# Row maxima of an attention score, taken from two PSUM banks by one VectorE instruction instead of two

## The reference

```
q = _lin(xn, Wq, bq).reshape(b, n, H, HD) / np.sqrt(HD)
k = _lin(xn, Wk, bk).reshape(b, n, H, HD)
score = jax.nn.softmax(jnp.einsum('bihd,bjhd->bhij', q, k), axis=-1)
v = _lin(xn, Wv, bv).reshape(b, n, R, HD)
out = jnp.einsum('bhij,bjrd->bihrd', score, v)
qv = _lin(xn, Wqv, bqv).reshape(b, n, H, 1, QK) / np.sqrt(QK)
comp = softmax(concatenate([qv, out], axis=-1) @ Ws.T + bs, axis=3)
out = (comp * out).sum(axis=3).reshape(b, n, DIM)
```

## Time and profile before

| what | value |
|---|---|
| median of 3 runs | 1427.76 us (1419.58 to 1430.48) |
| the profiled execution | 1429.73 us, span in the trace 1428.0 us |
| TensorE matmul | busy 1368.9 us (96%), 6333 instructions |
| VectorE | busy 1026.9 us (72%), 2050 instructions |
| GpSimd | busy 841.1 us (59%), 433 instructions |
| ScalarE | busy 756.1 us (53%), 1463 instructions |
| DMA | 48.35 MB, mean 34 GB/s |

### The profile page before, as it was taken

One profiled execution on the slowest core, in us unless ns is written; L12 is line 12 of the kernel. 1 busy time (PEld: TensorE's weight loads), 2 busy tenths in 40 slices (PEclk: granted clock), 3 DMA queues, 4 the chain that ended last, 5 costly groups with the idle time before them and its releaser, 6 DMA issues. The chain is left out here.

```text
span 1428.0 us, 23930 instructions
## 1 busy us (share of the span) xinstructions
PE 1368.9 (96%) x6333; PEld 436.7 (31%) x6333; DVE 1026.9 (72%) x2050; ACT 756.1 (53%) x1463; POOL 841.1 (59%) x433
## 2 busy tenths in 40 slices
PE   4699999999999999999999999999999999997898
PEld 3123222222222222222222222222222222223675
DVE  5745677877778686878777777768686868677852
ACT  4045555565555555555556555555555555563443
POOL 4235767576666766666757576665656565664321
PEclk9569999999999999999999999999999999999999
DMA  5200101010101001010101010100000000000000
GB/s 129 91 17 31 34 28 42 31 42 31 42 22 36 31 31 42 31 42 19 39 31 42 31 42 31 32 29 32 31 32 31 31 31 31 17 1 1 15 17 28
DMA packets 41937, 48.35 MB, mean 34 GB/s; under 512 B 4608, under 2 KB 23520, under 8 KB 41904
## 3 DMA queue, kind: packets, MB, share of 16 engines
q1 hardware_dynamic: 40770, 47.04, 10.0%
q0 software_dynamic: 352, 0.58, 0.3%
q10 hardware_dynamic: 782, 0.33, 0.1%
HBM read 22.51 MB, written 8.39 MB: 22 GB/s over the span
## 5 line engine op out<-in xcount | busy, mean ns | idle before, releaser
L1194 DVE TENSOR_REDUCE rowmax<-row_bank 128x1 f32<-128x512 f32 x1024 | 666.5, 684 | 319.9 <-PE row_bank L964 314.2
L1294 POOL TENSOR_TENSOR pair<-prob 128x1024 f32<-128x1024 f32 x256 | 603.8, 2359 | 452.0 <-ACT prob L1141 452.0
L1141 ACT ACTIVATE prob<-col_bank 128x512 f32<-128x512 f32 x1024 | 555.2, 594 | 463.9 <-PE col_bank L981 463.5
L989 PE MATMUL out_bank<-prob,v_op 128*64 128x512 f32 x2048 | 558.6, 624 | 0.0
L964 PE MATMUL row_bank<-k_op,q_op 72*128 72x512 bf16 x1024 | 323.6, 390 | 20.7 <-DMA v_op<-v_all 12.1
L981 PE MATMUL col_bank<-q_op,k_op 74*128 74x512 bf16 x1024 | 313.4, 387 | 0.1
L981 PEld LDWEIGHTS col_bank<-q_op,k_op 74*128 74x128 bf16 x1024 | 68.8, 98 | 332.2 <-ACT prob L1141 227.9
L989 PEld LDWEIGHTS out_bank<-prob,v_op 128*64 128x64 f32 x2048 | 101.9, 135 | 213.8 <-issue 200.5
L964 PEld LDWEIGHTS row_bank<-k_op,q_op 72*128 72x128 bf16 x1024 | 101.0, 99 | 167.6 <-DVE rowmax L1194 42.6
L999 PE MATMUL den_bank<-pair,onehot 128*32 128x512 f32 x1024 | 137.3, 608 | 0.0
L393 POOL TENSOR_TENSOR product<-mix_in,rows 128x2048 f32<-128x2048 f32 x16 | 72.5, 4529 | 2.1 <-POOLq L876 2.1
(11 more groups left out here) (183 smaller groups left out, 823.2 us busy)
## 6 DMA issues: line engine op xcount, KB each, us to landing
v_op<-v_all SPq DMA_DIRECT2D x64, 256.0 KB
k_op<-k_parts SPq DMA_DIRECT2D x64, 144.0 KB
q_op<-q_parts SPq DMA_DIRECT2D x192, 48.0 KB
q_parts<-along_parts SPq DMA_DIRECT2D x11, 192.0 KB, 2.2
k_parts<-along_parts SPq DMA_DIRECT2D x33, 64.0 KB, 2.1
out<-y_out SPq DMA_DIRECT2D x8, 256.0 KB, 2.3
q_op<-max_rows SPq DMA_DIRECT2D x64, 4.0 KB
q_parts<-first_parts SPq DMA_DIRECT2D x5, 192.0 KB, 2.1
```

What stands on the lines that cost most here:

```text
L989: last = nc.tensor.matmul(out_bank[slot % 2][ih * VW:(ih + 1) * VW, :], v_op[slot][:, t, :], halves(prob[:, t, :])[:, :, ih, :], start=(t ...
L1141: nc.scalar.activation(prob[:, t, h * HALF:(h + 1) * HALF], col_bank[h][:, :], ACT.Exp).then_inc(exp_done, 1)
L1194: nc.vector.tensor_reduce(rowmax[:, parity, t, h:h + 1], row_bank[h][:, :], AX.X, ALU.max).then_inc(max_done, 1)
L1294: pool.tensor_tensor(pair[:, k, :], prob[:, 2 * k, :], prob[:, 2 * k + 1, :], ALU.add).then_inc(pair_done, 1)
```

## The change

Both row banks become one PSUM tensor `row_banks` of 1024 columns (two banks), and `row_bank[0]` and `row_bank[1]` are its halves, so the matmuls write where they did. One `tensor_reduce` reads all 1024 columns and writes one maximum per query; it waits for both halves of the tile. `max_done` counts once per tile. TensorE waits once per tile, before the first half, that the reduction of tile t - 1 is done. `rowmax` loses its last dimension, so the reduction that negates the maxima reads 8 elements instead of 16. The steps of `split_max` come after the reduction: two of them after that of t = 0, one after that of t = 1.

```
-        rowmax = sb("rowmax", [P, 2, TB, 2])
+        rowmax = sb("rowmax", [P, 2, TB])
...
-        row_bank = [pb(f"row_bank{n}", [P, HALF]) for n in range(2)]
+        row_banks = pb("row_banks", [P, SEQ])
+        row_bank = [row_banks[:, n * HALF:(n + 1) * HALF] for n in range(2)]
...
             def row_scores(v, slot, t, known_free):
                 for h in range(2):
-                    if not known_free:
-                        pe.wait_ge(max_done, 2 * TB * v + 2 * t + h - 1)
+                    if not known_free and h == 0:
+                        pe.wait_ge(max_done, TB * v + t)
...
                         if last and (s, t) == (2, 0):
-                            pe.wait_ge(max_done, 2 * TB * U)
+                            pe.wait_ge(max_done, TB * U)
...
-            def row_max(v, parity, t, h):
-                dve.wait_ge(row_scored, 2 * TB * v + 2 * t + h + 1)
-                nc.vector.tensor_reduce(rowmax[:, parity, t, h:h + 1], row_bank[h][:, :], AX.X,
+            def row_max(v, parity, t):
+                dve.wait_ge(row_scored, 2 * TB * v + 2 * t + 2)
+                nc.vector.tensor_reduce(rowmax[:, parity, t:t + 1], row_banks[:, :], AX.X,
                                         ALU.max).then_inc(max_done, 1)
...
-                    dve.wait_ge(max_done, 2 * TB * w + 2 * TB)
-                    nc.vector.tensor_reduce(negmax[:, :], rowmax[:, parity, :, :], AX.X, ALU.max,
+                    dve.wait_ge(max_done, TB * w + TB)
+                    nc.vector.tensor_reduce(negmax[:, :], rowmax[:, parity, :].unsqueeze(2), AX.X, ALU.max,
                                             negate=True).then_inc(negmax_ready, 1)
...
-                        for h in range(2):
-                            if ahead:
-                                row_max(u + 2, s % 2, t, h)
-                            if 2 * t + h < 3 and not (last and s == SLOTS - 1):
-                                split_max(u + 1, (s + 1) % 2, 2 * t + h)
+                        if ahead:
+                            row_max(u + 2, s % 2, t)
+                        if not (last and s == SLOTS - 1):
+                            for step in {0: (0, 1), 1: (2,)}.get(t, ()):
+                                split_max(u + 1, (s + 1) % 2, step)
...
-                    for h in range(2):
-                        row_max(v, v, t, h)
+                    row_max(v, v, t)
```

## The result

The changed kernel takes 1473.59 us (median of 4 runs, 1469.45 to 1478.99), the kernel before beside it 1426.69; the ratio is 1.0337, with a 95% interval of 1.0284 to 1.039. The forecast was 1450 with a range of 1436 to 1466: right in sign, but the change cost 46.9 us where 22 were forecast. The profiled execution of the kernel after took 1478.99 us, with a span of 1477.2 against 1428.0.

The account below looks back on a forecast made before the run. It took TensorE to set the pace, VectorE counting only where TensorE waits for a bank. 8.4 us in the loop plus 13.6 ahead of group 0, 22.0, on 1429.73 gave 1451.7, taken as a median of 1450; range 1436 to 1466.

Parts of the forecast that it names:

- What bounds the kernel, and the margin of a plain tile: In the loop TensorE sets the pace; plain row pairs stay 1.98 us apart, the reduction fitting with 0.08 to spare.
- The merged reduction: One VectorE reduction of 1024 PSUM columns takes 1.21 us, as in SBUF, against 1.37 for two apart.
- Rival 3: Reading across two banks costs 1.37 us like two instructions, so every plain tile stalls 0.08: 1480 us, chance 0.10.
- The 82 us of VectorE's busy time: Over 512 merged reductions VectorE loses 82 us of busy time, 1.37 to 1.21 each, none on the path.
- Ahead of group 0: In the 16 tiles before group 0, matmuls and reduction form a chain, 2.34 us per tile against 1.42: 13.6 us more.
- The long steps: Around query part and weights TensorE's stalls grow 0.3 us each, 0.6 in each of 14 groups: 8.4 us.
- the 28 priced places: The query part and the weights in each of 14 groups, where TensorE stalls net 0.3 us longer.
- The two priced stalls of s = 2: Stalls at query part and weights: 0.6 and 0.61 us in along groups, against 0.32 each today; net 0.3 each.
- The clock: In group 0 the rise to 1.00 comes at the same work, first `denominators`, 13.6 us later, costing nothing further.
- Rival 2: The clock rises as soon as group 0 makes TensorE dense, 14.2 us less: 1436 us, chance 0.10.
- Rivals 4 and 5: 4: VectorE's saving reaches TensorE, 1414 us, chance 0.04. 5: the instruction is split again when built, chance 0.02.

Follow-up runs that it names:

- b1_sub_late: The kernel before, two reductions and two banks, with the subtraction of `split_max` behind the second row maximum of tile 1: 1445.71 us, ratio 1.015.
- a1_sub_ahead: The kernel after, with the subtraction of `split_max` ahead of the row maximum of tile 1 instead of behind it: 1447.19 us, ratio 1.0158.
- a5_all: The kernel after with early subtraction and the old start, plus query part, shift and weights ahead of their tiles' row maxima: 1537.28 us, ratio 1.0772.
- a6_sub_first: a5_all with the subtraction of `split_max` put ahead of the query part in tile 1: 1427.48 us, ratio 0.9993 to the kernel before.

## Why the prediction was wrong

- **What bounds the kernel, and the margin of a plain tile**: right. The loop grows by what TensorE's row pairs come late behind the held subtraction (0.74 us in the tile above), and plain row pairs in the kernel after stand 1.98 apart.
- **The merged reduction**, 1.21 us: right, 1.22. Rival 3, two banks as dear as two instructions, is out. The 82 us of VectorE's busy time that it was to save were too many, though: the two reductions of a pair overlap (1.29 us together, not 1.37), and the page's busy time goes from 666.5 to 625.2, 41 us.
- **Ahead of group 0**, 13.6 us: right, 13.9; undone by itself it came back.
- **The long steps**, 8.4 us: here it failed, in one sentence, "with the steps of `split_max` most are shorter" than the margin of 0.9. The subtraction was entered at 0.07 us, its price in its old place, though the change moves it from between two reductions to behind the merged one. In its new place it runs beside GpSimd's addition and lasts 1.84 us, and VectorE has 0.9. That is so in 61 of its 64 executions, in all four units of a group, and not in the 28 priced places. The trace of before held the warning. Its old place is only some 0.06 us ahead of the addition, and in the first unit of group 0, at the lower clock, it came behind the addition's start:

```profile
69.86 2.04 DVE L1208 TENSOR_TENSOR max_parts<-negmax,max_parts 128x8 bf16<-128x8 f32 x1
...
69.54 2.34 POOL L1294 TENSOR_TENSOR pair<-prob 128x1024 f32<-128x1024 f32 x1 [23.23 <-ACT prob L1141]
```

  Three short operations of 256 columns, too, took 1.66 to 1.96 us on average where 0.42 is their own length. I read their lengths as theirs. Moved back, some 28 of the loop's 32.4 us left.
- **The two priced stalls of s = 2**: right in kind, twice too large. With the subtraction early an along group takes 77.13 instead of 76.80, 0.33 and not 0.6. A held instruction ends with GpSimd's addition or soon behind it (0.02 us behind for 8 columns, 0.28 for 256), however late it starts: the query part's mean fell from 1.96 to 1.90 us, where I moved a fixed 2.11 along. In the kernel after itself the stall at the query part is 0.56 us, near the 0.6 of the prediction, but by luck: the subtraction in front of it takes the hold, and the query part lasts 0.41.
- **The clock**: I tied its rise to the first `denominators`. Wrong. In the kernels before (rise at 96.3, first `denominators` at 94.0) and after (112.3 and 108.8) it came soon behind them, but it rose at 73.9 in b1_sub_late and at 92.1 in a1_sub_ahead, ahead of their first `denominators` (85.1 and 101.3):

```profile
67.60:73.90 6.30, 6.30 (x15) 1.26 (x13) 5.15 (x17) 3.04 (x6) 2.93 (x2) 0.50 0.07 27
73.90:90.00 16.10, 16.10 (x70) 3.99 (x69) 11.00 (x26) 9.05 (x19) 8.51 (x8) 1.00 0.01 2
```

  It comes 7 us after group 0 begins in b1_sub_late (66.8 to 73.9) and 33 in the kernel after (79.4 to 112.3), with nearly the same work. At 0.47 us a microsecond this is 12 us between executions, about the spread of a kernel's runs; and of the kernel before, the runs of 1418 to 1421 us have a mean granted clock of 0.982 to 0.984, those from 1429 on 0.974 to 0.976. Rival 2 (a rise as soon as TensorE is dense) is nearly met in b1_sub_late and not in the kernel after; what decides it stays open. In the profiled pair the rise comes 2.6 us later after the start of group 0, worth 1.2 us; the other 1.4 of the 2.6 us of group 0 I put down to its own held subtractions, which no run shows by themselves.
- **Rivals 4 and 5**: VectorE's saving did not make the kernel faster, and 512 merged reductions were run.

## What to carry to other kernels

When an edit moves a VectorE instruction with two SBUF inputs, however small, look at what GpSimd runs at its new moment: here it was held to the end of GpSimd's instruction, and what counted was how much of that one was left. An operation whose duration in the trace is far above that of its like elsewhere may be held; compare its end with the ends of GpSimd's instructions. If it is, its price is that of its place and not its own length. Merging two instructions also moves what stood between them and takes away the second buffer's slack, so price the neighbours as well as the pair.

## What the runs showed that I had not expected

- A VectorE `tensor_tensor` of 256 columns takes 0.42 us alone and 1.5 to 2.2 when it starts while GpSimd's addition of 1024 columns (2.36 us) is running; one of 8 columns goes from 0.16 to 1.85.
- Every standstill of TensorE of 2.73 us in a loop that is otherwise dense cost it the full clock, mostly for 13.7 us; of those of 1.9 us nine in 14 did; with stalls of at most about 1 us the loop never lost it. In a5_all the along groups take 85.3 us, and 76.8 in a6_sub_first, where only the order of two short instructions differs: 8.5 us for a stall of some 3.
- TensorE was dense at half clock in group 0 for 7 us in one execution and for 33 in another of nearly the same program.
